# A depthwise convolution kernel with its long filters fetched in strips of 8 rows

## The chip, the cores and the metric

The kernel runs on one core of a Trainium2 chip. Times are device microseconds (us) of one execution, launch excluded; the value quoted for the kernel before is the median of 3 runs. Besides these there is one profiled execution, from which all rows below come.

## The reference

The input x is 32 images of 192 channels of 56 x 56, in float32. Two blocks follow each other. Each normalises over groups of 6 channels (32 groups), convolves every channel with a filter of its own (depthwise), and adds the result to its input. The first filter is 31 x 31 with a bias, the second is 11 x 11 and is computed from a few coordinates and weights.

```
x = x + conv31x31_depthwise(group_norm(x)) + bias
x = x + conv11x11_depthwise(group_norm(x))
```

## The kernel before

A channel's convolution is done on TensorE as products with banded (Toeplitz) matrices: the image rows stand on the partitions, two partitions per row (the two parities of columns), and one matrix for each shift of columns holds the taps of the vertical direction. The matrices are not built on chip for each channel. At the start the taps of all channels are laid out in DRAM (`padded1`, `padded2`), and each channel's matrices are fetched as overlapping windows of that padded row: partition after partition reads the same taps shifted by one cell of 16 bytes. A long filter (31 x 31) has 28 such matrices, a short one (11 x 11) has 9; each convolution issues every matrix product three times, for float32 precision from high and low parts: 84 matmuls a long convolution, 27 a short one.

The image has 56 rows in four bands of 16, 16, 16 and 8 rows (`BANDS`, `HB`, `HB_LAST`). `load_toeplitz` (L545) fetches a filter by one DMA for each band and each half `e` (high part, low part): 8 DMAs. A band's DMA covers only the columns that its rows can reach (`windows`): band 0 has 31 cells of 16 bytes, so runs of 496 B; band 1 has 46, 736 B; band 2 has 39, 624 B; band 3 has 23, 368 B. The short filters are fetched by the same function with 336, 416, 416 and 208 B. There are two places for a long filter and two for a short one (`T_RING`), so a filter is issued when the convolution before the one before it, of the same kind, has ended.

The work runs over 32 groups of 6 channels. An iteration has 12 slots, long and short convolutions in turn. All transfers of the loop are issued by SyncE, in this order for each slot: wait until the convolution just before has ended (`conv_done`), issue the next filter of its kind; in two slots of the twelve also store half a group of results (4 DMAs, L555), and in one load the images of the group after next (4 DMAs, L533). SyncE's program is a loop over 28 of the groups; the others stand before and behind it, written out. TensorE waits for a filter's landing (`landed`) before the convolution's first matmul. VectorE, ScalarE and GpSimd normalise, transpose and split the images.

Of the kernel before, what the change touches and what calls it, by code (L numbers as in the profile page):

```python
# [42 lines left out]
B, C, H, W = 32, 192, 56, 56  # L43
GROUPS = 32
CG = C // GROUPS
BANDS = 4
HB = 16
HB_LAST = H - (BANDS - 1) * HB
# [23 lines left out]
K1, K2 = 31, 11  # L72
# [5 lines left out]
T_RING = 2  # L78
# [16 lines left out]
class Filter:  # L95


    def __init__(self, K, first_pair):
        self.K = K
        self.pad = K // 2  # L100

        self.first_pair = first_pair
        self.offset = -1 - 2 * first_pair
        self.d0 = -((self.pad + self.offset + 1) // 2)
        self.D = (self.pad - self.offset + 1) // 2 - self.d0 + 1
        assert self.d0 % 2 == 0 and self.D % 2 == 0
        self.ms = range(self.d0 // 2, self.d0 // 2 + self.D // 2)
        self.halved = self.D // 4 if first_pair else 0
        self.sums = self.D // 2 + self.halved
        self.sum_steps = 3 if self.halved else 2  # L110
        self.L = self.D + self.sums
        self.cell = 4
        self.slab = H * self.cell
        self.block = self.L * self.slab
        self.windows = []
        for q in range(BANDS):
            first, last = HB * q, min(H, HB * q + HB) - 1
            self.windows.append((max(0, first - self.pad), min(H - 1, last + self.pad) + 1))
        self.margin = HB - 1
        self.period = (K + self.margin) * self.cell  # L120
        self.padded = self.L * self.period + self.margin * self.cell
# [27 lines left out]
def slots(i):  # L149

    if not isinstance(i, int) or 2 <= i < GROUPS:
        return list(range(SLOTS))
    return [s for s in range(SLOTS) if 0 <= channel(i, s)[1] < GROUPS]


def channel(i, s):

    conv, c = PATTERN[s]
    return conv, (i if conv == FIRST else i - 2 if s in LATE_SLOTS else i - 1), c


def job(i, s):

    if isinstance(i, int) and not 2 <= i < GROUPS:
        return sum(len(slots(k)) for k in range(i)) + slots(i).index(s)
    return i * SLOTS + (s + CG - 2 - SLOTS)


def ring(i, s, size):

    return job(i if isinstance(i, int) else 2, s) % size
# [10 lines left out]
def place(i, s):  # L182

    if isinstance(i, int) and i >= GROUPS:
        return PLACES[(job(i, s) - (GROUPS * SLOTS - LAST_SHORT)) % 3]
    return PLACES[PATTERN[s][1] % F_PLACES] if PATTERN[s][0] == FIRST else PLACES[F_PLACES]
# [76 lines left out]
def positive(value):  # L263

    return not isinstance(value, int) or value > 0


def conv_norm_kernel(nc, x, weight1, bias, coord, radius, weight2, out):
    f1, f2 = Filter(K1, -1), Filter(K2, 0)

    with ExitStack() as ctx:
        def sb(name, shape, dt=F32):
# [239 lines left out]
        def band_rows(q):  # L512
            return HB if q < BANDS - 1 else HB_LAST
# [16 lines left out]
        def _(sp):  # L530
# [3 lines left out]

            def load_toeplitz(m, place, f, padded, toep, landed):

                for q in range(BANDS):
                    (lo, hi), rows = f.windows[q], band_rows(q)
                    first = HB - rows
                    for e in range(2):  # L540
                        src = bass.AP(padded, m * (2 * f.padded) + e * f.padded + (lo - HB * q + f.pad + first) * f.cell,
                                      [[f.cell, rows], [f.period, f.L], [1, (hi - lo) * f.cell]])
                        slabs = toep[2 * (HB * q + first) + e:2 * HB * (q + 1):2, place, :].rearrange(
                            "p (k n) -> p k n", n=f.slab)
                        sp.dma_start(slabs[:, :, lo * f.cell:hi * f.cell].bitcast(F32), src).then_inc(landed[place], 16)  # L545

            def load_toeplitz1(m, place):
                load_toeplitz(m, place, f1, padded1, toep1, toep1_landed)

            def load_toeplitz2(m, place):  # L550
                load_toeplitz(m, place, f2, padded2, toep2, toep2_landed)
# [667 lines left out]
        @block.tensor  # L1219
        def _(pe):  # L1220
            pe.wait_ge(acc_zeroed, 1)

            def toeplitz(toep, f, place, part, k):

                return bass.AP(toep, place * f.block + k * f.slab + part, [[T_RING * f.block, P], [2, M]])

            def convolve(i, s, f, toep, place_of_toep):

                n, at, p = job(i, s), place(i, s), ring(i, s, P_RING)
                done = [p2_done, None, u_done, None, conv_done] if f.halved else [p2_done, None, conv_done]  # L1230
                before_outer = 3 if f.halved else 1
                for k, (bank, column, start, shift, held, count, matrices) in enumerate(f.products()):
                    if k == before_outer:
                        pe.wait_ge(lo_ready, n + 1)
                        if positive(n + 1 - P_RING):
                            pe.wait_ge(image_ready, n + 1 - P_RING)

                    def outputs(m):
                        return max(0, -(m + shift)), min(count, held - (m + shift))

                    matrices = sorted(matrices, key=lambda x: outputs(x[0])[0] - outputs(x[0])[1])
                    for m, w in matrices:
                        j0, j1 = outputs(m)
                        dst = acc[0:M, p, bank, (column + j0) * B:(column + j1) * B]
                        cols = slice(at + (start + j0 + m + shift) * B, at + (start + j1 + m + shift) * B)
                        for part, src in ((0, x_hi), (0, x_lo), (1, x_hi)):
                            last = nc.tensor.matmul(dst, toeplitz(toep, f, place_of_toep, part, w), src[:, cols],  # L1247
                                                    start=(m == matrices[0][0] and part == 0 and src is x_hi),
                                                    stop=(m == matrices[-1][0] and part == 1), skip_group_check=True)
                    if done[k] is not None:  # L1250
                        last.then_inc(done[k], 1)

            def iteration(i):
                for s in slots(i):
                    n = job(i, s)
                    pe.wait_ge(lo_inner_ready, n + 1)
                    if positive(n + 1 - P_RING):
                        pe.wait_ge(y_ready, n + 1 - P_RING)
                    conv, g, c = channel(i, s)
                    f, toep, landed = (f1, toep1, toep1_landed) if conv == FIRST else (f2, toep2, toep2_landed)  # L1260

                    pe.wait_ge(landed[c % T_RING], g * (16 * 2 * BANDS * CG // T_RING) + 16 * 2 * BANDS * (c // T_RING + 1))
                    convolve(i, s, f, toep, c % T_RING)

            iteration(0)
            iteration(1)
            with pe.Fori(2, GROUPS) as i:
                iteration(i)
            iteration(GROUPS)
            iteration(GROUPS + 1)  # L1270
# [21 lines left out]
```

## Time and profile before

| | us |
|---|---|
| median of 3 runs (lowest, highest) | 3523.25 (3522.18, 3523.5) |
| the profiled execution's own time | 3523.46 |
| its span, first to last instruction | 3521.7 |
| TensorE busy | 3431.3 (97%) |
| VectorE busy | 3146.4 (89%) |
| DMA queue of SyncE, share of the 16 engines | 86.2% |

The DMA share adds up the time of packets that overlap on an engine, so it can pass 1 when all 16 are in use. Issuing instructions of SyncE's queue ("SPq") are not counted as busy on the page, but the timeline shows each with its duration. A row of the timeline merges neighbouring instructions of one kind. "PE" is TensorE, L545 is line 545 of the kernel.

### The profile page before, as it was taken

What the parts mean: (1) busy time and instruction counts of PE and PEld (TensorE: products, weight loads), DVE (VectorE), ACT (ScalarE), POOL (GpSimd) and SP (SyncE); (2) the same over time, 40 slices, a digit from 0 to 9 for tenths busy, and PEclk for the clock granted to TensorE, in tenths of its full rate; (3) what the DMA queues carried; (4) which work ended last, traced back from release to release, by engine and by line L of the source; (5) the groups of instructions that cost most, each with busy time, mean ns of one, the idle gap of its engine ahead of it and who ended that gap; (6) DMA issues with size and microseconds to landing.
All of it is one profiled execution on the core that took longest, in us unless ns stands there. A gap on an engine that the chain in (4) does not pass through costs nothing.

```text
span 3521.7 us, 66355 instructions
## 1 busy us (share of the span) xinstructions
PE 3431.3 (97%) x21312; PEld 3268.3 (93%) x21312; DVE 3146.4 (89%) x4671; ACT 1294.2 (37%) x1634; POOL 1202.3 (34%) x840
## 2 busy tenths in 40 slices
PE   5899999999999999999999999999999999999997
PEld 4789999999999999999999999999999999999996
DVE  7899998899988999998999988999989999989987
ACT  3233333333333333333333333333333333333333
POOL 6213333333333333333333333333333333333332
PEclk9899999999999999999999999999999999999999
DMA  8998888898888898888898888998888988889773
GB/s 182 185 200 160 172 161 166 175 180 167 163 169 168 165 181 167 162 164 173 168 176 170 161 164 173 176 170 168 164 166 171 184 164 162 169 169 183 137 134 86
DMA packets 896128, 587.51 MB, mean 167 GB/s; under 512 B 501656, under 2 KB 858136, under 8 KB 895576
## 3 DMA queue, kind: packets, MB, share of 16 engines
q1 hardware_dynamic: 895416, 585.62, 86.2%
q14 instruction: 152, 1.25, 0.1%
q10 hardware_dynamic: 544, 0.38, 0.1%
q8 instruction: 16, 0.26, 0.0%
HBM read 499.20 MB, written 86.61 MB: 166 GB/s over the span
## 4 chain that ended last, share of the span: by engine, by line
PE 93%; issue 2%; SPq 2%; DVE 1%; DMA 1%; POOL 0%; ACT 0%; POOLq 0%; DVEq 0%; ACTq 0%
PE acc L1247 93%; SPq L545 2%; DMA toep<-padded 1%; DMA padded<-raw 0%; SPq L555 0%; SPq L571 0%; DVE yt L1040 0%; DVE acc L1031 0%; DVE raw L1086 0%; DVE acc L1071 0%; DVE raw L1049 0%; DVE raw L1062 0%; POOL raw L709 0%; POOL raw L706 0%; POOL xt L748 0%
## 5 line engine op out<-in xcount | busy, mean ns | idle before, releaser
L1247 PE MATMUL acc<-x_hi,toep 128*112 128x224 f32 (+5 forms) x14208 | 3306.9, 323 | 83.4 <-DMA toep<-padded 70.5
L1247 PEld LDWEIGHTS acc<-x_hi,toep 128*112 128x112 f32 x14208 | 2383.3, 182 | 193.5 <-issue 80.6
L1247 PE MATMUL acc<-x_lo,toep 128*112 128x224 f32 (+5 forms) x7104 | 2301.0, 324 | 0.0
L1247 PEld LDWEIGHTS acc<-x_lo,toep 128*112 128x112 f32 x7104 | 1290.9, 182 | 52.5
L751 POOL TENSOR_TENSOR xt<-xt 128x960 f32<-128x960 f32 x188 | 425.9, 2265 | 1117.8 <-DVE xt L989 1117.8
L788 ACT ACTIVATE x_hi<-xt 128x768 fp32r<-128x768 f32 (+1 forms) x384 | 279.2, 727 | 1093.4 <-POOL xt L747 573.3
L1031 DVE TENSOR_TENSOR acc<-acc,yt 128x896 f32<-128x896 f32 x384 | 418.7, 1090 | 227.4 <-PE acc L1247 226.2
L746 POOL TENSOR_TENSOR xt<-xt 128x512 f32<-128x512 f32 x180 | 233.1, 1295 | 1094.3 <-DVE xt L989 1094.3
L791 ACT ACTIVATE x_hi<-xt 128x960 fp32r<-128x960 f32 x384 | 386.9, 1008 | 573.1 <-POOL xt L751 324.1
L989 DVE STREAM_TRANSPOSE xt<-images 128x960 f32<-128x960 f32 x384 | 452.5, 1178 | 34.9 <-ACT images L775 6.6
L775 ACT ACTIVATE images<-raw,norm 128x896 f32 (+1 forms) x384 | 439.8, 1145 | 88.2 <-DVE norm L969 88.2
L1049 DVE TENSOR_TENSOR raw<-yt,raw 128x896 f32 (+1 forms) x384 | 421.5, 1098 | 30.3 <-DVE yt L1040 12.9
L1014 DVE TENSOR_TENSOR x_lo<-xt,x_hi 128x960 fp32r<-128x960 f32 x384 | 442.6, 1152 | 2.2 <-ACT x_hi L791 0.2
L980 DVE BATCH_NORM_STATS2 part<-raw 96x6 f32 (+3 forms) x768 | 443.3, 609 | 0.0
L1040 DVE STREAM_TRANSPOSE yt<-acc 128x896 f32<-128x896 f32 x384 | 424.9, 1107 | 9.5
L748 POOL TENSOR_TENSOR xt<-xt 128x960 f32<-128x960 f32 x180 | 409.7, 2276 | 0.0
L1008 DVE TENSOR_TENSOR x_lo<-xt,x_hi 128x768 fp32r<-128x768 f32 (+1 forms) x384 | 301.4, 785 | 0.0
L803 ACT ACTIVATE yt<-acc 128x448 f32<-128x448 f32 x192 | 104.0, 542 | 204.1 <-DVE raw L1049 192.2
L1021 DVE TENSOR_TENSOR yt<-acc,yt 128x448 f32<-128x448 f32 x192 | 114.4, 596 | 26.9 <-ACT yt L800 26.9
L807 ACT ACTIVATE small<-small 32x1 f32<-32x1 f32 x64 | 12.9, 202 | 233.8 <-DVE small L945 233.8
L800 ACT ACTIVATE yt<-acc,bias_all 128x224 f32<-128x224 f32 x192 | 85.8, 447 | 15.7 <-DVE raw L1049 1.2
L943 DVE BATCH_NORM_AGGREGATE small<-yt 32x2 f32<-32x252 f32 x64 | 81.9, 1280 | 0.9
(58 smaller groups left out, 407.9 us busy)
## 6 DMA issues: line engine op xcount, KB each, us to landing
toep<-padded SPq DMA_DIRECT2D x384, 322.0 KB
toep<-padded SPq DMA_DIRECT2D x384, 273.0 KB
toep<-padded SPq DMA_DIRECT2D x384, 217.0 KB
out_dram<-raw SPq DMA_DIRECT2D x189, 336.0 KB, 5.6
raw<-in_x_dram SPq DMA_DIRECT2D x93, 672.0 KB, 11.7
toep<-padded SPq DMA_DIRECT2D x768, 58.5 KB
toep<-padded SPq DMA_DIRECT2D x384, 80.5 KB
toep<-padded SPq DMA_DIRECT2D x384, 47.2 KB
```

The source lines that it names most:

```text
L748: nc.gpsimd.tensor_tensor(differences_held(), shifted_even(), repeated_odd(), ALU.subtract).then_inc(xd_ready, 1)
L751: nc.gpsimd.tensor_tensor(differences_held(), repeated_odd(), shifted_even(), ALU.subtract).then_inc(xd_ready, 1)
L775: nc.scalar.activation(image(ring(i, s, I_RING))[:, :, 1:1 + W], raw_rows(g, c), ACT.Identity, bias=norm[:, 0:1], scale=norm[:, 1:2]).then ...
L791: nc.scalar.activation(high_part, source, ACT.Copy).then_inc(hi_ready, 1)
L980: nc.vector.bn_stats(parts[0:held, k, c, :], raw_channel(g, c)[0:held, k * HALF:(k + 1) * HALF]).then_inc(parts_ready, 1)
L989: nc.vector.transpose(transposed(), blocks(image(ring(i, s, I_RING)))[:, :, ::-1, :]).then_inc(xt_ready, 1)
L1008: nc.vector.tensor_tensor(low_part, source, high_part.bitcast(F32), ALU.subtract).then_inc(lo_inner_ready, 1)
L1014: nc.vector.tensor_tensor(low_part, source, high_part.bitcast(F32), ALU.subtract).then_inc(lo_ready, 1)
L1031: nc.vector.tensor_tensor(outer(i, s), outer(i, s), p2.unsqueeze(1).to_broadcast([P, 2, JH * B]), ALU.add).then_inc(y_ready, 1)
L1040: nc.vector.transpose(yt[:].rearrange("p (i s b) -> p s i b", s=2, b=B), outer(i, s).rearrange("p s (i b) -> p s i b", b=B)).then_inc(imag ...
L1049: nc.vector.tensor_tensor(rows, yt[:].rearrange("p (j h e) -> p h j e", h=HB, e=2), rows, ALU.add).then_inc(residual_added, 1)
L1247: last = nc.tensor.matmul(dst, toeplitz(toep, f, place_of_toep, part, w), src[:, cols], start=(m == matrices[0][0] and part == 0 and src i ...
```

## The change

Each long filter's bands 1 and 2 are each fetched in two strips of 8 rows, of which each has its own, narrower window of columns. A long filter is then 12 DMAs: band 0 with 16 rows (496 B runs), band 1 with two times 8 rows (608 B), band 2 with 8 rows of 496 B and 8 rows of 608 B, band 3 with 8 rows (368 B), each for `e` = 0 and 1. Short filters keep their 8 DMAs. TensorE waits for the matching count (`one` = 16 x 2 x number of strips).

```
-        self.windows = []
+        self.strips = []
         for q in range(BANDS):
-            first, last = HB * q, min(H, HB * q + HB) - 1
-            self.windows.append((max(0, first - self.pad), min(H - 1, last + self.pad) + 1))
+            first = HB - HB_LAST if q == BANDS - 1 else 0
+            while first < HB:
+                rows = min(HB // 2 if q in split_bands else HB, HB - first)
+                low = HB * q + HB - first - rows
+                high = low + rows - 1
+                self.strips.append((q, first, rows, max(0, low - self.pad), min(H - 1, high + self.pad) + 1))
+                first += rows
...
-    f1, f2 = Filter(K1, -1), Filter(K2, 0)
+    f1, f2 = Filter(K1, -1, (1, 2)), Filter(K2, 0, ())
...
-                for q in range(BANDS):
-                    (lo, hi), rows = f.windows[q], band_rows(q)
-                    first = HB - rows
+                for q, first, rows, lo, hi in f.strips:
                     for e in range(2):
                         src = bass.AP(padded, m * (2 * f.padded) + e * f.padded + (lo - HB * q + f.pad + first) * f.cell,
                                       [[f.cell, rows], [f.period, f.L], [1, (hi - lo) * f.cell]])
-                        slabs = toep[2 * (HB * q + first) + e:2 * HB * (q + 1):2, place, :].rearrange(
+                        slabs = toep[2 * (HB * q + first) + e:2 * (HB * q + first + rows):2, place, :].rearrange(
                             "p (k n) -> p k n", n=f.slab)
                         sp.dma_start(slabs[:, :, lo * f.cell:hi * f.cell].bitcast(F32), src).then_inc(landed[place], 16)
...
-                    pe.wait_ge(landed[c % T_RING], g * (16 * 2 * BANDS * CG // T_RING) + 16 * 2 * BANDS * (c // T_RING + 1))
+                    one = 16 * 2 * len(f.strips)
+                    pe.wait_ge(landed[c % T_RING], g * (one * CG // T_RING) + one * (c // T_RING + 1))
```

What SyncE issues for one long filter inside its loop, in the kernel before (rows x matrices x elements of 4 bytes; `ISA` and `REGISTER_ALU` set addresses):

```order
L545 DMA toep1<-padded1 16x28x124
L545 ISA
L545 DMA toep1<-padded1 16x28x124
L545 REGISTER_ALU
L545 DMA toep1<-padded1 16x28x184
L545 ISA
L545 DMA toep1<-padded1 16x28x184
L545 DMA toep1<-padded1 16x28x156 x2
L545 ISA
L545 DMA toep1<-padded1 8x28x92
L545 ISA
L545 DMA toep1<-padded1 8x28x92
```

And the same place in the changed kernel:

```order
L548 DMA toep1<-padded1 16x28x124
L548 ISA
L548 DMA toep1<-padded1 16x28x124
L548 ISA
L548 DMA toep1<-padded1 8x28x152
L548 ISA
L548 DMA toep1<-padded1 8x28x152 x3
L548 DMA toep1<-padded1 8x28x124 x2
L548 DMA toep1<-padded1 8x28x152 x2
L548 DMA toep1<-padded1 8x28x92 x2
```

The four DMAs of 16 rows for bands 1 and 2 have become eight of 8 rows; band 0 and band 3 are as they were, and nothing moved past another instruction. The order on TensorE, VectorE, ScalarE and GpSimd is the same in both kernels.

## Rows read from the trace of the kernel before

**Rows 1.** The page of the kernel before: section 1 and section 4.

```profile
PE 3431.3 (97%) x21312; PEld 3268.3 (93%) x21312; DVE 3146.4 (89%) x4671; ACT 1294.2 (37%) x1634; POOL 1202.3 (34%) x840
...
PE 93%; issue 2%; SPq 2%; DVE 1%; DMA 1%; POOL 0%; ACT 0%; POOLq 0%; DVEq 0%; ACTq 0%
```

**Rows 2.** Middle stretch: length, engines busy, clock, DMA share, GB/s.

```profile
250.00:3440.00 3190.00, 3190.00 (x19914) 3042.71 (x19913) 2877.98 (x4283) 1189.05 (x1496) 1102.10 (x718) 1.00 0.87 167
```

**Rows 3.** Waits of TensorE over the whole span: in total, times, longest.

```profile
PE acc L1247 <- DMA toep<-padded: 70.5, 11, 39.6
```

**Rows 4.** Line L545, which issues the filter loads: its register moves.

```profile
L545 SPq MOVE toep<-padded x2688: 29/29/38, 251.9 to 3235.4; - x192
```

**Rows 5.** Timeline of SyncE's queue, one iteration: start, us, what.

```profile
1493.23 2.01 SPq L533 DMA_DIRECT2D raw<-in_x_dram  x4
1495.45 33.26 SPq L545 DMA_DIRECT2D toep<-padded  x32
1529.00 3.61 SPq L555 DMA_DIRECT2D out_dram<-raw  x4
1540.82 41.12 SPq L545 DMA_DIRECT2D toep<-padded  x48
1582.32 3.52 SPq L555 DMA_DIRECT2D out_dram<-raw  x4
1586.14 13.29 SPq L545 DMA_DIRECT2D toep<-padded  x16
1599.92 0.35 SPq L533 DMA_DIRECT2D raw<-in_x_dram  x1
```

**Rows 6.** SyncE queue waits: 250 to 3440; 3235 to 3440; 1486 to 1593.

```profile
SPq L545 <- PE acc L1247: 113.0, 42, 6.6
SPq L621 <- PE acc L1247: 11.5, 1, 11.5
...
SPq L545 <- PE acc L1247: 42.4, 9, 6.6
...
SPq L545 <- PE acc L1247: 2.4, 1, 2.4
```

**Rows 7.** L545 from 1548.9 (four 16-row), from 1491.1 (two 8-row): min/median/max ns.

```profile
L545 SPq DMA_DIRECT2D toep<-padded x4: 580/580/581, 1548.9 to 1551.1; - x4
...
L545 SPq DMA_DIRECT2D toep<-padded x2: 702/709/716, 1491.1 to 1492.0; - x2
```

**Rows 8.** Timeline of SyncE's queue, stretch 500 to 607.

```profile
519.31 13.33 SPq L545 DMA_DIRECT2D toep<-padded  x16
...
535.56 33.48 SPq L545 DMA_DIRECT2D toep<-padded  x32
```

**Rows 9.** Windows as in Rows 2: under 16-row strips, under 8-row strips.

```profile
33.00:34.00 1.00, 0.00 (x0) 0.00 (x0) 1.00 (x2) 0.84 (x1) 0.93 (x1) 1.00 1.19 209
...
2586.40:2586.90 0.50, 0.50 (x5) 0.49 (x4) 0.50 (x2) 0.00 (x0) 0.38 (x1) 1.00 0.64 125
453.30:453.60 0.30, 0.30 (x4) 0.30 (x3) 0.05 (x1) 0.00 (x0) 0.30 (x1) 1.00 0.62 103
```

**Rows 10.** Issues of filter loads by size, the long filters' four bands.

```profile
toep<-padded SPq DMA_DIRECT2D x384, 322.0 KB
toep<-padded SPq DMA_DIRECT2D x384, 273.0 KB
toep<-padded SPq DMA_DIRECT2D x384, 217.0 KB
toep<-padded SPq DMA_DIRECT2D x384, 80.5 KB
```

**Rows 11.** The chain that ended last, 26 to 40: start, us, what.

```profile
29.50 0.62 SPq L545
30.16 0.74 SPq L545
30.95 8.53 DMA toep<-padded
```

More of the change, by code:

```diff
@@ L95, with __init__ @@
 class Filter:
-    def __init__(self, K, first_pair):
+    def __init__(self, K, first_pair, split_bands):
         self.K = K
```

## The prediction

> **What bounds the kernel now.** I read the page first, then stretches of busy time, then TensorE's waits, and last the queue of SyncE, which the page leaves out of the busy times. TensorE is busy 97% of the span and has 93% of the chain that ended last [rows 1]. Between 250 and 3440 us it has no gap: 3190 us busy of 3190, 19914 matmuls, at full granted clock [rows 2]. A long and a short convolution together are 84 + 27 = 111 matmuls, so the pair takes 3190 x 111 / 19914 = 17.8 us, and an iteration of six pairs 106.7 us. All its waits for filters are 70.5 us in 11 times, one of them the 39.6 us ahead of the first convolution [rows 3]. By this view filter transfers cost nothing in the long middle, and a change of them could cost nothing either. That is where one must look at the engine which issues them.
>
> One iteration of SyncE's queue goes from the image load at 1493.23 to the next at 1599.92, again 106.7 us [rows 5]. The issue rows add up to 96.8 us: 33.26 + 41.12 + 13.29 = 87.7 for the 96 filter DMAs, 2.01 + 3.61 + 3.52 for images and results. Between rows there are five small gaps (1.6 us) and one of 8.2 us, from 1532.6 to 1540.8. Is that slack? The waits say no: in a stretch that holds it SyncE waited for TensorE once, for 2.4 us [rows 6]. It lies behind the store that ends the loop body, so I take it for the jump back of SyncE's loop, which a busier queue pays just the same. SyncE's own need is thus 106.7 - 2.4 = 104.3 us of every 106.7. Over 250 to 3440 its waits for TensorE are 113.0 + 11.5 us, of which 42.4 + 11.5 fall behind 3235, where the loop has ended [rows 6]; the other 70.6 us over 28 iterations are 2.5 us each, so the one iteration is typical. The 28 comes from the loads' register moves, one per filter DMA of the loop: 2688 / 96, in 251.9 to 3235.4 [rows 4].
>
> So there are two engines at the limit, TensorE with no gap and SyncE with 2.5 us. What hides a later filter is not the average but the two places per kind: a filter is issued three convolutions ahead, which allows a lag of some 20 us once, not in each iteration.
>
> **The change part by part.** TensorE, VectorE, ScalarE and GpSimd keep their instructions. SyncE loses four 16-row issues for each long filter and gains eight of 8 rows; bytes and engines of the transfers change too.
>
> Issue time. Four 16-row issues take 580 ns each and start 0.73 us apart (2.2 us for three steps) [rows 7], so bands 1 and 2 cost 2.9 us now. An 8-row issue takes 702 to 716 ns, so it is longer and not shorter than one of 16 rows [rows 7]; outside the loop, 0.74 against 0.62 us, it is the same [rows 11]. The step to the next is more than the issue. The two of rows 7 start 0.9 us apart, with address instructions between them, and the bare gap in the chain is 0.04 us (29.50 + 0.62 to 30.16) [rows 11]. In the changed order only the first of the eight has address instructions ahead of it beyond its move of 29 ns [rows 4], so I take 0.71 + 0.09 = 0.80 us a step, with 0.75 and 0.90 as the ends. Eight steps are 6.4 us; the long filter grows by 6.4 - 2.9 = 3.5 us (3.1 to 4.3), an iteration by 21.0 us (18.6 to 25.8).
>
> Nothing hides that. 104.3 + 21.0 = 125.3 us against the 106.7 that TensorE needs: SyncE becomes the bound, and each iteration is 18.6 us longer. Over 28 iterations this is 521 us. The wait moves to TensorE, which will stand before filters that are still to land.
>
> Stalls of the queue. Two pairs that stand behind an image load took 33.26 us for 32 DMAs, and 33.48 in another iteration [rows 5, 8], where an undisturbed pair takes 13.29 or 13.33 for 16 [rows 5, 8]. The 6.6 us too many are SyncE held up while the images move. I keep them as they are: the same four image loads meet about the same rest of a long filter. The ends are that they vanish (118.7 us an iteration) or grow by some 5 us, as they may with more DMAs in flight.
>
> The engines that carry the bytes. The issue sizes fall from 322 to 133 KB for half of band 1 and from 273 to 108.5 and 133 KB for band 2 [rows 10] (8 rows x 28 runs x 608 or 496 B), in bytes 1785 KB to 1609 KB a long filter, 10% less. But the rate is lower. Under 16-row strips the DMA share is 1.19 and 209 GB/s, under 8-row strips 0.64 and 125 GB/s [rows 9]: by the share, half of the engines carry it. So the four transfers of band 1 and 2 now take 1190 KB / 209 = 5.8 us, and the eight of the change 1014 KB / 125 = 8.3 us, on the eight engines that also have band 3. Per long filter these have 2.1 (band 0) + 8.3 + 1.3 (band 3, 161 KB at 125) = 11.7 us; per short filter about 1.9 (357 KB at 209 or slower); per iteration also 4.8 MB of images and results (6 channels of 32 images, in and out), 23 us at 209. Sum 6 x 13.6 + 23 = 105 us of 125: close, but not what ends last.
>
> The Trainium skill, DMA: Bandwidth & Descriptors, section on why a DMA increments its semaphore by 16, says that a DMA of the hardware queues uses the largest number of engines up to 16 that divides its slowest dimension, and that the issuing sequencer itself writes the rest of the count. By this rule 8 rows use 8 engines and cost an extra write at the issue. The trace agrees on both sides, by the share of 0.64 against 1.19 and the 0.71 against 0.58 us. The rule speaks against this change, and the price is that of the rows above.
>
> The first and last stretches. Ahead of the first matmul the filter is issued and lands 8.53 us behind its last issue [rows 11]; four more issues add about 3.3 us there. Of the chain up to 250 us I count about five long filters whose issue or landing TensorE waits for, and one loopless iteration that already runs with SyncE short: 17 to 27 us, I take 20. Behind the loop SyncE waits 53.9 us in its two last full iterations [rows 6], more than the 42 us that come on top: nothing.
>
> Sum: 3523.46 (the profiled execution's own time, the median is 3523.25) + 521 + 20 = 4064 us.
>
> **The rivals.** (1) The stalls of the queue go, since it is SyncE that is late and no longer the transfers: 118.7 us an iteration, 28 x 12.0 + 20 = 356, 3880 us. For it speaks that DMAs are issued more slowly against their work; against it, that the image load is a burst which four quick issues start at once (2.01 us for all, rows 5).
>
> (2) The eight engines are the bound as well, and stall the issue of each long filter. In another window the 8-row strips moved at 103 GB/s [rows 9]. Then the eight take 10.1 us, a long filter 2.1 + 10.1 + 1.6 = 13.8 us on these engines against 2 x 0.8 + 10 x 0.8 = 9.6 of issue. If half of the difference comes back to SyncE as stalls, 2 us a filter, an iteration is 137 us, and the kernel 3523 + 28 x 30.6 + 20 = 4400 us. For it speaks the DMA share of 0.87 already [rows 2]; against it that short filters, 6.4 us to issue and 1.9 to move, drain the queue each time.
>
> (3) Not slower: TensorE remains the bound. The place is SyncE's queue in the loop; it holds if the added issue time stays under 2.5 us of wait plus the 6.6 us of stalls, 9.1 us an iteration or 1.5 a filter, so if an 8-row step costs at most (2.9 + 1.5) / 8 = 0.55 us. Then only the smaller transfers count: the 11 waits for landings [rows 3] get shorter by 10% of some 8 us each, 9 us, and the kernel takes 3514 us. Both 8-row issues in rows 7, at 0.70 us and more, speak against it, and so does the one in rows 11.
>
> The same page of the Trainium skill, section Issuing engines are not separate DMA queues, holds that the time to initiate DMAs is usually small beside the DMA. By that rule the time would stay, as in (3). The trace differs here: 13.3 of 17.8 us of a pair are issue.
>
> **How the numbers follow.** Forecast 0.78; (1) 0.11; (2) 0.07; (3) 0.04, of which half faster and half within what can't be told. This kernel's measurement tells 0.2% from no change, 7 us. The forecast's own spread is 0.75 to 0.90 us a step: 122.9 to 130.1 us an iteration, 3997 to 4200 us. Cases (1) and part of (2) widen it to 3840 to 4230. Faster 0.02, same 0.02, slower 0.96.
>
> **What the changed profile would show.** TensorE with waits "<- DMA toep<-padded" of 400 to 600 us in some hundreds of times, busy near 85%. SyncE's waits for TensorE in the loop near zero. A pair without images 16.8 us for 20 DMAs in the timeline of its queue, an iteration near 125 us from image load to image load. 8-row issues with a median of 700 ns or more. DMA share lower than 0.87, because time is longer and half of the engines idle. SPq L548 in the chain with a large share. The forecast is wrong if an 8-row issue takes under 0.6 us, if the 8.2 us gap at the loop's end shrinks (then it was slack after all, and an iteration is 117 us), or if the filters issue in time and TensorE keeps its 17.8 us a pair.

## The result and the profile after

The changed kernel takes 4080.9 us (median of 4 runs, 4075.91 to 4084.84), the kernel before 3522.72 (4 runs, 3521.42 to 3523.5). The ratio is 1.1583, with a 95% interval of 1.1569 to 1.1597: 558 us slower. The forecast was 4064 us in a range of 3840 to 4230. The time fell in the range, and the main mechanism held: the queue of SyncE became the bound. Several sizes in the sum were off. Those inside the loop nearly cancelled, so it is partly luck that the forecast came out as near as it did.

The page of the changed kernel, sections 1, 3 and 4, against [rows 1]:

```profile
PE 3580.7 (88%) x21312; PEld 3386.9 (83%) x21312; DVE 3150.1 (77%) x4671; ACT 1289.0 (32%) x1634; POOL 1195.7 (29%) x840
...
q1 hardware_dynamic: 895416, 551.22, 68.6%
q14 instruction: 153, 1.25, 0.1%
...
SPq 78%; issue 14%; PE 6%; DMA 1%; DVE 1%; ACT 0%; DVEq 0%
```

TensorE had 93% of the chain and has 6%. The queue of SyncE has 78%. VectorE, ScalarE and GpSimd are busy within 7 us of before. TensorE has the same 21312 matmuls, but is busy 149 us longer, at a lower clock (below).

The middle stretch, columns as in [rows 2]:

```profile
260.00:3750.00 3490.00, 3115.57 (x18569) 2948.89 (x18568) 2690.99 (x4009) 1102.66 (x1393) 1019.06 (x669) 0.94 0.69 135
```

TensorE now has gaps of 3490.00 - 3115.57 = 374 us where it had none [rows 2]. DMA is less busy than before, 0.69 against 0.87, although the queue that feeds it is the bound. On the mean of the 16, the DMA engines have more room than before. How full the eight are that carry an 8-row strip, this share doesn't show.

The waits, over the whole span, of TensorE and then of SyncE (in total, times, longest):

```profile
PE acc L1250 <- DMA toep<-padded: 472.1, 101, 42.8
...
SPq L548 <- PE acc L1250: 33.6, 10, 9.1
```

The roles have changed. TensorE waited 70.5 us for filters [rows 3] and waits 472.1. SyncE waited for it 113.0 us in the stretch from 250 to 3440 [rows 6]; of the 33.6 us that are left none lies between 260 and 3750.

One iteration of SyncE's queue (start, us, what), against [rows 5]:

```profile
1603.91 17.07 SPq L548 DMA_DIRECT2D toep<-padded  x20
1621.49 2.37 SPq L538 DMA_DIRECT2D raw<-in_x_dram  x4
1624.06 40.00 SPq L548 DMA_DIRECT2D toep<-padded  x40
1664.35 4.04 SPq L558 DMA_DIRECT2D out_dram<-raw  x4
1674.16 49.72 SPq L548 DMA_DIRECT2D toep<-padded  x60
1724.26 3.76 SPq L558 DMA_DIRECT2D out_dram<-raw  x4
1728.32 17.44 SPq L548 DMA_DIRECT2D toep<-padded  x20
1746.28 2.24 SPq L538 DMA_DIRECT2D raw<-in_x_dram  x4
```

From image load to image load it is 1746.28 - 1621.49 = 124.8 us, where it was 106.7. The filter issues are 40.00 + 49.72 + 17.44 = 107.2 us of it, 19.5 more than the 87.7 of before. The gap behind the store that ends the loop body is 1674.16 - 1668.39 = 5.8 us.

The issues of a long filter's 8-row strips, and five 16-row issues of a short filter some 10 us later (min/median/max in ns), against [rows 7]:

```profile
L548 SPq DMA_DIRECT2D toep<-padded x5: 697/697/710, 1574.5 to 1577.8; - x5
...
L548 SPq DMA_DIRECT2D toep<-padded x5: 580/581/609, 1584.2 to 1587.1; - x5
```

Four steps from 1574.5 to 1577.8 are 0.82 us each. The 16-row issue has kept its 0.58 us; that of 8 rows costs 0.70. All eight 8-row issues of this filter take 6.5 us, from 1574.5 to the start of band 3 at 1581.0.

**Where the 552 us of the two profiled spans lie.** The filter loads' register moves mark the loop, as in [rows 4]; in the changed kernel they are

```profile
L548 SPq MOVE toep<-padded x3360: 29/29/42, 293.4 to 3792.5; - x198
```

The loop starts 293.4 - 251.9 = 41.5 us later. It lasts 3499.1 us in place of 2983.5, 515.6 more. What lies behind it is 281.6 in place of 286.3 us, 4.7 less. Over 28 iterations it is 125.0 us each, and 106.6 before. The column "iteration" below comes from this row of each kernel.

### The profile page after: what moved, and what is told of

It is laid out like the page before. It is cut to its first block, busy times and chain, and to the rows that moved or that the text cites. A ratio compares the mean times of both kernels' runs of the same rounds, so it can differ in the third digit from the quotient of the medians.

```text
span 4074.1 us, 67459 instructions
## 1 busy us (share of the span) xinstructions
PE 3580.7 (88%) x21312; PEld 3386.9 (83%) x21312; DVE 3150.1 (77%) x4671; ACT 1289.0 (32%) x1634; POOL 1195.7 (29%) x840
## 4 chain that ended last, share of the span: by engine, by line
SPq 78%; issue 14%; PE 6%; DMA 1%; DVE 1%; ACT 0%; DVEq 0%
SPq L548 71%; PE acc L1250 6%; SPq L558 5%; SPq L538 2%; DMA toep<-padded 1%; SPq L624 0%; DMA padded<-raw 0%; SPq L574 0%; SPq L644 0%; DVE raw L1089 0%; DVE acc L1074 0%; DVE yt L1043 0%; DVE acc L1034 0%; DVE raw L1052 0%; DVE raw L1065 0%
## 5 line engine op out<-in xcount | busy, mean ns | idle before, releaser
L1250 PE MATMUL acc<-x_hi,toep 128*112 128x224 f32 (+5 forms) x14208 | 3455.8, 332 | 486.4 <-DMA toep<-padded 472.1
L1250 PEld LDWEIGHTS acc<-x_hi,toep 128*112 128x112 f32 x14208 | 2486.4, 190 | 627.9 <-DMA toep<-padded 382.7
L1250 PE MATMUL acc<-x_lo,toep 128*112 128x224 f32 (+5 forms) x7104 | 2360.2, 332 | 0.0
L1250 PEld LDWEIGHTS acc<-x_lo,toep 128*112 128x112 f32 x7104 | 1352.9, 190 | 52.0
```

## The experiments

Three theories stood beside each other. By issue time: SyncE's queue ends last, and its time is the sum of its issues. By the engines: the eight DMA engines that carry 8-row strips end last, or hold the queue up. By the loop's end: a part of SyncE's time is the gap behind the loop's last instruction, and depends on where the loop's code lies. Each ratio is to runs of the kernel before that were taken beside it.

| kernel | us | ratio, 95% | iteration, us |
|---|---|---|---|
| changed kernel | 4080.9 | 1.1569 to 1.1597 | 125.0 |
| e1_short_strips | 3771.14 | 1.0683 to 1.0718 | 115.0 |
| e2_band2_only | 3609.55 | 1.023 to 1.0265 | 109.0 |
| e3_wide_strips | 4381.31 | 1.2407 to 1.2449 | 134.6 |
| e4_matrix_halves | 3699.42 | 1.048 to 1.0515 | 113.1 |
| e5_loop_at_0 | 3928.12 | 1.1129 to 1.1166 | 119.6 |
| e6_act_issues_band2 | 3821.36 | 1.0831 to 1.0867 | 115.6 |
| e7_before_loop_at_0 | 3522.8 | 0.999 to 1.0009 | 106.5 |
| e8_images_spread | 4156.86 | 1.1773 to 1.1812 | 127.7 |
| e9_act_and_spread | 3710.46 | 1.0511 to 1.0546 | 111.5 |
| e10_spread_loop_at_0 | 4009.9 | 1.1368 to 1.1406 | 122.2 |
| e11_quarter_images | 3874.06 | 1.0974 to 1.1011 | 117.9 |
| e12_act_quarter_images | 3560.74 | 1.009 to 1.0124 | 106.3 |

**e1: the short filter is split in place of the long one.**

```diff
-    f1, f2 = Filter(K1, -1, (1, 2)), Filter(K2, 0, ())
+    f1, f2 = Filter(K1, -1, ()), Filter(K2, 0, (1, 2))
```

> The short filters instead of the long ones have bands 1 and 2 in strips of 8 rows (12 DMAs a short filter, 8 a long one). The strips of a short filter carry a sixth of a long one's bytes. If the number and kind of SyncE's issues sets the time, SyncE has as many issues an iteration as in the changed kernel: 4080 us, within 40. If the eight engines and the bytes on them set it, the engines gain under 1 us a pair over the kernel before and have room: 3523 to 3550 us.

It gave 3771.14 us, which is in neither range. A part of its queue's timeline:

```profile
1603.41 2.12 SPq L538 DMA_DIRECT2D raw<-in_x_dram  x4
1605.84 37.54 SPq L548 DMA_DIRECT2D toep<-padded  x40
1643.68 3.54 SPq L558 DMA_DIRECT2D out_dram<-raw  x4
1647.96 48.84 SPq L548 DMA_DIRECT2D toep<-padded  x60
...
1701.01 16.59 SPq L548 DMA_DIRECT2D toep<-padded  x20
```

There are as many issues as in the changed kernel, so issue time alone doesn't explain the time. Half of the 10.0 us that an iteration is shorter is the loop's end: 1643.68 + 3.54 to 1647.96 is 0.7 us, not 5.8. The rest lies in the rows of filters, 37.54 + 48.84 + 16.59 = 103.0 against 107.2 us, and in shorter store rows. The strips of the short filter carry fewer bytes, and the stall behind the image load is smaller too: 37.54 - 2 x 16.59 = 4.4 us against 40.00 - 2 x 17.07 = 5.9.

**e2: band 2 alone is split** (`Filter(K1, -1, (2,))`), ten transfers a long filter.

> Of the long filters only band 2 is split in strips of 8 rows: 10 DMAs a long filter. SyncE's issue as the cause: half of the 21 us that the full change adds to an iteration, so 104.3 + 10.5 = 114.8 us, less up to 2 us that the changed kernel's loop end was shorter; 28 x 6 to 8 us and 10 at the start: 3700 to 3760 us. Engines as the cause: they need about 99 us of 106.7 an iteration, no change: 3523 to 3540 us.

It gave 3609.55 us, outside both ranges. Here too the loop ends in 0.7 us:

```profile
1580.24 4.03 SPq L558 DMA_DIRECT2D out_dram<-raw  x4
1585.01 44.64 SPq L548 DMA_DIRECT2D toep<-padded  x54
```

5.0 us less in 28 iterations are 141 us; 3610 + 141 = 3751 lies in the range that the issue time gave. Two kernels now had a short end of the loop, where nothing at that place had been edited but the number of issues in the code.

**e5: the changed kernel with the loop's first instruction of SyncE at slot 0 of its instruction buffer; e7: the kernel before, likewise.** Neither touches an instruction of the loop's work.

```diff
-            with sp.Fori(2, GROUPS - 2) as i:
+            with nc.Fori(2, GROUPS - 2, engines=bass.OrderedEngineSet([sp.engine]), head_slot={sp.engine: 0}) as i:
```

> The changed kernel, with the first instruction of SyncE's loop placed at the start of a block of 256 instructions; nothing else differs. In the traces so far SyncE's queue stood 5.4 us an iteration behind the loop's branch in the changed kernel, but 0.3 us in the two kernels with other lengths of code. If SyncE's queue is the bound and this gap is the code's placement, it falls to 0.3 us and the time by 28 x 5.1 = 143 us: 3938 us, within 15. If the engines that carry the bytes are the bound, the gap only becomes a wait elsewhere: 4080 us.

> The kernel before, with SyncE's loop placed at the start of a block in the same way. TensorE has no gap there, so the 5 us that SyncE gains an iteration are hidden: 3523 us, within 5. If SyncE's lag costs something now and then, up to 10 us less.

Both came as expected: 3928.12 us, 153 less than the changed kernel, and 3522.8, no difference. The queue of e5 around the loop's end:

```profile
1576.02 40.39 SPq L548 DMA_DIRECT2D toep<-padded  x40
1616.71 4.07 SPq L558 DMA_DIRECT2D out_dram<-raw  x4
1621.46 28.46 SPq L548 DMA_DIRECT2D toep<-padded  x34
```

The gap is 0.7 us. So it is neither slack nor a fixed price: it depends on where the loop's code lies. In e7 the gap has gone from the 8.2 us of [rows 5] to 0.7 as well, and SyncE only waits longer for TensorE, over the whole span 354.8 us where the kernel before has 155.6. Its timeline and its waits:

```profile
1528.84 4.01 SPq L555 DMA_DIRECT2D out_dram<-raw  x4
1533.58 47.49 SPq L545 DMA_DIRECT2D toep<-padded  x48
...
SPq L545 <- PE acc L1247: 354.8, 96, 9.6
```

The new waits lie in the row of filters, 47.49 us where it was 41.12.

A gain on an engine that isn't the bound is worth nothing (e7), and the same gain is worth 153 us where it is (e5). This pair is the plainest evidence that SyncE's queue became the bound. The Trainium skill, Runtime: NRT & Kernel Launch, section Instruction fetch mechanics, says that a taken branch to an instruction outside the two pages at hand makes the engine fetch the page before it goes on. The traces agree. The page of a profile lists the packets that bring instructions as "q14 instruction" (packets, MB, share). The kernel before, e5 and e7 have

```profile
q14 instruction: 152, 1.25, 0.1%
...
q14 instruction: 20, 0.16, 0.0%
...
q14 instruction: 17, 0.14, 0.0%
```

and the changed kernel 153. The page doesn't name the engine that they are for, but e7 differs from the kernel before in nothing but the place of SyncE's loop. Nearly all of them fall into the loop: between 300 and 3235 us there are 138 in the kernel before and 3 in e7. Some lie in the gap itself, two in that of the kernel before (1532.62 to 1540.82) and one in that of the changed kernel (1668.39 to 1674.16):

```profile
q14 instruction: 2, 0.02, 0.5%
...
q14 instruction: 1, 0.01, 0.3%
```

The two in the kernel before start 2.2 us apart, at 1536.8 and 1539.1 us, so the one that is not there any more accounts for most of the 2.4 us by which the gap shrank. e1, e2, e6, e9, e10 and e12 have a gap of 0.7 us and no such packet in the stretches looked at (1500 to 1800 us); e3, e4, e8 and e11 have both.

**e3: 8-row strips with as many columns as the whole band needs**, so as many issues and more bytes.

```diff
-                high = low + rows - 1
-                self.strips.append((q, first, rows, max(0, low - self.pad), min(H - 1, high + self.pad) + 1))
+                band, end = HB * q, min(H, HB * q + HB) - 1
+                self.strips.append((q, first, rows, max(0, band - self.pad), min(H - 1, end + self.pad) + 1))
```

> As the changed kernel, 12 DMAs in the same strips, but each strip of bands 1 and 2 as wide as its whole band (736 and 624 B runs in place of 608 and 496): 14% more bytes in these eight transfers. SyncE's issue as the cause: 4080 us, within 20. Bytes on eight engines as the cause: 1190 KB in place of 1015 KB at 125 GB/s are 1.4 us more a long filter, 4300 to 4350 us.

It gave 4381.31 us, 300 more than the changed kernel, above the 4300 to 4350 that the bytes on the engines gave, and far from the 4080 of issue time. The queue's timeline:

```profile
1592.96 18.64 SPq L548 DMA_DIRECT2D toep<-padded  x20
1612.09 2.93 SPq L538 DMA_DIRECT2D raw<-in_x_dram  x4
1615.23 43.38 SPq L548 DMA_DIRECT2D toep<-padded  x40
1658.90 3.88 SPq L558 DMA_DIRECT2D out_dram<-raw  x4
1668.60 54.15 SPq L548 DMA_DIRECT2D toep<-padded  x60
```

Each row of filters is longer than its like in the changed kernel, 1.6 us a pair even where no images move. (The edit also gives SyncE 12 more address instructions an iteration, at some 0.04 us each: 0.5 of the 9.6 us.) The median of L548's issues is 697 ns, 692 in the changed kernel. What grew is the number of issues over 800 ns, from 13.7 to 24.4 an iteration. So issue time isn't a fixed price for each issue. The queue is still what ends last (it has 80% of the chain), but how long it takes depends on how fast the transfers that it has issued get done: with more bytes on eight engines it is held up.

**e4: bands 1 and 2 in halves of 14 matrices, all 16 rows**: twelve transfers as well, and all engines take part.

```diff
+                            half = f.L // 2
+                            for h in range(2):
+                                part = bass.AP(padded, m * (2 * f.padded) + e * f.padded + h * half * f.period
+                                               + (lo - HB * q + f.pad + first) * f.cell,
+                                               [[f.cell, rows], [f.period, half], [1, (hi - lo) * f.cell]])
...
```

> 12 DMAs a long filter as in the changed kernel, but bands 1 and 2 are cut by their matrices (14 and 14 of 28) and not by rows: every DMA of these has 16 rows and so all engines, and the old windows. SyncE's issue as the cause, with 0.12 us less for each of eight issues: 124.8 - 5.8 = 119.0 us an iteration, 28 x 5.8 + 6 = 168 us less than the changed kernel: 3912 us, within 40. Eight engines in use as the cause: gone here, 3523 to 3540 us.

It gave 3699.42 us, 213 less than issue time gave, and 160 more than the engines gave. Two rows of its eight issues, undisturbed and behind an image load:

```profile
1643.86 5.58 SPq L554 DMA_DIRECT2D toep<-padded  x8
...
1586.71 6.75 SPq L554 DMA_DIRECT2D toep<-padded  x8
```

5.58 us for eight, where the changed kernel needs 6.5, and 1.2 us of stall. This splits the loss in two: four more issues a long filter cost 176 us, and that they are of 8 rows the other 381 (part of it by the gap, which is 4.4 us here). "More transfers" was the smaller part, "in shorter runs of rows" the larger. The parts belong to this order of adding them: the first 2.4 us an iteration that SyncE loses are free, since it waits as long for TensorE [rows 6].

**e6: ScalarE issues the four strips of band 2** from the third group on, so that SyncE has eight of the twelve.

```diff
+                    if not (peeled and i < 2):
+                        strips_of_band2(i, s)
...
```

> The changed kernel's transfers, all in the same strips, but from the third group on the four of band 2 of each long filter are issued by ScalarE's queue: 8 issues a long filter are left to SyncE. SyncE's queue as the bound: it needs 24 x 0.81 = 19.4 us less an iteration, 105.9 against TensorE's 106.7, so TensorE bounds again: 3523 plus some 20 for the start, 3535 to 3580 us. The bytes on eight engines as the bound: unchanged, 4080 us. If it is both, through the stalls of the issuing queue, between the two.

It gave 3821.36 us, in between, so both causes are at work. This kernel has the short loop end (0.7 us), so the fair comparison is e5: 107 us less, not 260, and still in between. SyncE has time again, and TensorE still waits; its waits and SyncE's over the span, and those of TensorE from 1530 to 1545:

```profile
PE acc L1276 <- DMA toep<-padded: 291.5, 43, 43.0
...
SPq L550 <- PE acc L1276: 497.1, 100, 7.8
...
PE acc L1276 <- DMA toep<-padded: 6.2, 1, 6.2
```

There is one late landing in the iteration, in the filters behind the image load. ScalarE's own queue is held up there too: of its four issues behind that load the longest took 4.5 us.

```profile
L909 ACTq DMA_DIRECT2D toep<-padded x4: 691/698/4454, 1517.7 to 1520.2; - x4
```

So the stall is not a matter of SyncE's queue alone. 6.2 us are less than the 115.6 - 106.6 = 9.0 that the iteration has too many. Most of the rest is the clock (the wait and the 7.1 us behind it, columns as in [rows 2]):

```profile
1531.64:1537.86 6.22, 0.01 (x1) 0.03 (x1) 5.96 (x11) 1.39 (x2) 2.21 (x1) 0.82 0.71 151
1537.86:1545.00 7.14, 7.14 (x43) 7.01 (x44) 4.53 (x5) 2.57 (x4) 3.00 (x3) 0.68 0.70 107
```

TensorE is at the 1.2 GHz level for (1 - 0.82) x 2 x 6.22 = 2.2 us at the end of the wait, which cost nothing more, and for (1 - 0.68) x 2 x 7.14 = 4.6 us of work behind it, which cost half of that, 2.3. 6.2 + 2.3 = 8.5 us, near the 9.0 that are to be explained.

**e8, e9, e10: the four image loads apart**, one each in slots 7 to 10 of the iteration: with the changed kernel, with e6, and with e5.

```diff
...
-                        load_x(i + 2)
+                        load_x(i + 2, [0])
+                    if s in (8, 9, 10) and not (isinstance(i, int) and (i == 0 or i + 2 >= GROUPS)):
+                        load_x(i + 2, [s - 7])
```

> The changed kernel, with the four image loads of an iteration issued one in each of four slots and not all in one. In the changed kernel the two pairs behind the image load take 40.0 us to issue and not 2 x 17.1: 5.9 us of stall. If these stalls are time of SyncE's queue that the bound includes, they go: 125.3 - 5.9 = 119.4 us an iteration, 4081 - 165 = 3916 us, within 40. If the sum of the engines' work is the bound, it is unchanged: 4080 us.

> ScalarE issues the four strips of band 2, as in the run before, and the image loads are spread over four slots. That run had left one TensorE wait of 6.2 us an iteration behind the image load and one stretch of 6.8 us at half clock after it. If the filters are late there because they queue behind 2.4 MB of images, both go, and TensorE bounds: 3821 - 28 x 9.2 = 3563 us, within 25. If strips of 8 rows are too slow on their engines wherever they stand, the wait only moves: 3750 to 3821 us.

> The changed kernel, all issues on SyncE, with both the spread image loads and the loop at the start of a block. If SyncE's queue is still the bound, the two gains add up: 125.3 - 5.1 - 5.9 = 114.3 us an iteration, 3928 - 165 = 3763 us, within 40. If the eight engines' work is what is left, it stays above 3850 us.

e8 gave 4156.86 us, 76 more than the changed kernel: a miss, and on the wrong side. The burst was not what made the stall. Two of its twelve-issue rows, each behind one image load:

```profile
1535.90 14.32 SPq L548 DMA_DIRECT2D toep<-padded  x12
...
1558.48 15.67 SPq L548 DMA_DIRECT2D toep<-padded  x12
```

Twelve issues of a long filter take some 10 us undisturbed. The stall moved with the loads, and now two filters paid. e10 gave 4009.9 us, a miss too: 147 less than e8, about the 153 that e5 gained by the loop's place. So spreading costs about the same in both (76 and 82 us), and the two effects add. e9, where SyncE has room, gained 111 us on e6 but stayed 147 above what was expected; TensorE's waits were 208.1 us in 66 times. These are shorter waits, 3.2 us in the mean against 291.5 / 43 = 6.8 in e6.

**e11 and e12: SyncE's loop loads a quarter of the images' rows**, in the changed kernel and in e6. All issues stay, and three quarters of the loop's image bytes go. These two kernels leave out work that the result needs and serve for the time alone.

```diff
-                    sp.dma_start(raw_band(g, q, 0, CG), dram_band(x_dram, g, q, 0, CG)).then_inc(x_landed, 16)
+                    n = band_rows(q) * W // (1 if isinstance(g, int) else 4)
+                    sp.dma_start(raw_band(g, q, 0, CG)[:, :, 0:n], dram_band(x_dram, g, q, 0, CG)[:, :, 0:n]
+                                 ).then_inc(x_landed, 16)
```

> The changed kernel, but SyncE's loop loads only the first quarter of each band's rows of the images; the rest of the image buffer keeps older data. The number and the place of all issues are the same, the engines have 1.8 MB less to move in an iteration. Spreading the image loads made the time longer (4157 us), so the stalls don't come from their standing together; if they come from the bytes of images that share the eight engines with the strips, the 11.4 us of stalls an iteration fall by 6 to 9 us: 4081 - 28 x 7.5 = 3870 us, 3830 to 3915. If the stalls belong to the 8-row strips alone, 4050 to 4080 us.

> The run with ScalarE issuing the four strips of band 2, with the same quarter of the images. What was left of SyncE's queue there was one wait of TensorE an iteration behind the image load. If the images' bytes ahead of a filter cause it, an iteration is TensorE's 106.7 us: 3821 - 28 x 9.2 = 3563 us, within 25. If the strips of 8 rows are too slow on eight engines by themselves, 3700 us or more.

Both came as expected: 3874.06 us, 207 less than the changed kernel, and 3560.74. In the timeline of e11 the filters behind the image load take

```profile
1551.09 2.17 SPq L539 DMA_DIRECT2D raw<-in_x_dram  x4
1553.46 32.96 SPq L550 DMA_DIRECT2D toep<-padded  x40
```

less than two undisturbed pairs (34.1 us), in place of 40.00. So the stall behind the image load is the work of the image bytes. It is 7.0 of the 7.1 us that an iteration got shorter. In e12, where ScalarE issues a part of the filter as well, the landings are back in time, TensorE waits 100.2 us in all, and SyncE's queue goes at TensorE's pace, 106.8 us from image load to image load:

```profile
PE acc L1278 <- DMA toep<-padded: 100.2, 14, 41.6
...
1529.40 2.12 SPq L539 DMA_DIRECT2D raw<-in_x_dram  x4
...
1636.22 2.12 SPq L539 DMA_DIRECT2D raw<-in_x_dram  x4
```

With a part of SyncE's issues and the bytes before the filters both taken away, and the short loop end that this kernel has too, the loss of the change is 38 us in place of 558. No kernel beat the one before, which e7 equals.

## Why the prediction was right, step by step

- *TensorE and SyncE both at the limit, no gap and 2.5 us*: right, and the base of all else. e7 confirms TensorE's side: with 7.5 us less at SyncE's loop end nothing changed in the time, and SyncE's waits grew by 199 us, 7.1 an iteration.
- *Issue time, 0.80 us a step, 3.5 us a long filter, 21.0 an iteration*: right for the issues themselves. One takes 0.70 us, and the eight of a filter 6.5 us, where 6.4 were forecast. (That only the first of the eight has address instructions ahead was misread: by the order list the second has them too.) Over an iteration the filter rows without the stall and the wait for TensorE went from 87.7 - 6.6 - 2.4 = 78.7 to 107.2 - 5.9 = 101.3 us, 22.6 more. So the term is 1.6 us short. Some issues are longer than the rest in pairs without images too (1.06 us for the one at 1581.0, against 0.70), and e3, which has more of these, points to the eight engines' pace.
- *28 iterations, 18.6 us each, 521 us*: 28 x 18.4 = 515.6 by the register moves. It came out so near because errors cancel: filters 1.6 us more than forecast, the rows of images and results 1.0 more (10.2 in place of 9.1), against the stall 0.7 less and the gap 2.4 less. That is 125.3 - 0.5 = 124.8 us.
- *The stalls of the queue stay at 6.6 us*: 5.9. The size was near, but the reason given ("a burst which four quick issues start at once") fell with e8. What holds the queue up is how many bytes the engines have before them: with a quarter of the image bytes it is gone (e11, -207 us), with wider 8-row strips it grows everywhere (e3, +300 us), and with all engines on each strip it is nearly gone (e4).
- *The 8.2 us gap is SyncE's jump, which a busier queue pays just the same*: that it is no slack was right, and the decision against "an iteration is 117 us" hung on it. That it stays the same was wrong: 5.8 us after, 0.7 in e1, e2 and e5. The prediction named this as a sign that it is wrong, with the gap as slack and an iteration of 117 us. The sign came and its meaning did not, since an iteration took 125. By the packets of the instruction queue the gap is a fetch of code, with one packet fewer in the changed kernel. The placement of the loop is worth 153 of the 558 us, and the prediction named no such risk; had the edit moved the loop's head to a good place, the forecast would have been 136 us too high (4064 - 3928), though still in its range.
- *The eight engines, 105 us of 125: close, but not what ends last*: right for the end, but they were not without effect. Rival (2) had a correct mechanism (the engines' pace comes back to SyncE as stalls) with a price too high for this size of strip; in e3, with more bytes, it comes near its number.
- *The start, 20 us*: 41.5. The first filter was right, TensorE's first wait grew from 39.6 to 42.8 us against the 3.3 predicted. What was mis-sized is how many filters are paid for ahead of the loop. By the timelines of both queues 208 filter issues stand there in place of 152, so 14 long filters have grown, where the prediction counted about five and one iteration. At 3.8 us each that is 53 us. SyncE's waits for TensorE ahead of the loop went from 29.2 to 14.5 us and gave 14.7 back, which leaves 38. *Behind the loop nothing*: -4.7 us.
- *Rival (1), 3880 us*, is nearly e11's 3874.06: the stalls do have that price, but it takes fewer bytes to be rid of them. *Rival (3), 3514 us*, fell with the issue of 0.70 us. With it fell, for this kernel, what the Trainium skill says in DMA: Bandwidth & Descriptors, section Issuing engines are not separate DMA queues, that the time to initiate a DMA is usually small beside it.
- *TensorE busy near 85%, waits of 400 to 600 us in some hundreds of times*: 88%, and 472.1 us in 101 times, fewer than forecast. The busy share is higher than forecast since its clock fell, which was not foreseen: the mean over the span is 0.941, so (1 - 0.941) x 2 x 4074 = 480 us at the half clock, and the same matmuls were busy 3580.7 - 3431.3 = 149 us longer. It lies in time in which TensorE would have waited; that it adds to the time where SyncE has room was seen in e6 alone.

What stays open: the parts don't add up to one ledger. The loop's place (-153), the image bytes (-207), issues moved to ScalarE (-260, the short loop end included) overlap, and how many bytes or transfers may be under way before the queue is held up was not measured. Nor is it shown why four loads apart, with the same bytes, cost more than four at once (e8).

## What to carry to other kernels

Look at the queue that issues before you split transfers: if it has as little to spare as the busiest engine, each added DMA is paid in full, in each iteration, however little the engine tables say of it. Cut a transfer so that the number of its rows (its slowest dimension) stays the same: here halves by matrix cost 176 us and halves by rows 558. And where a queue with a loop is the bound, look at the gap behind its last instruction; it may be the place of the code, and cheaper to mend than anything in the body. The count of instruction packets on the page of the profile tells: 152 and 153 with the gap, 17 and 20 without.

## What the runs showed that was not expected

- The gap at the end of a loop on SyncE was 8.2 us in the kernel before, 5.8 in the changed one, 4.4 in e4 and 0.7 in e1, e2, e5 and e7. In the iterations looked at, the long gaps have packets of the instruction queue in them and the short ones have none.
- A queue's time per issue isn't a constant: 20 issues of a pair took 16.59 us (e1), 17.07 (changed) and 18.64 (e3), with more bytes in the 8-row strips each time, and with no wait for any other engine in it.
- Four loads apart stall the queue more than four at once (e8, +76 us), as long as the queue is the bound.
- In e6, behind a wait of 6.2 us, TensorE worked at the 1.2 GHz level for 4.6 us, so a late landing cost about 1.4 times itself.
